# Attention and mixture of experts of a first layer, from two programs one after the other to one program of interleaved steps

## The reference, cut to what matters

```python
h = _layernorm(x) * (1 + ca) + sa
x = x + ga * attention0(h)      # 16 heads of 8, rope, causal, softmax, output projection
h = _layernorm(x) * (1 + cb) + sb
x = x + gb * ffn0(h)

def ffn0(x):                    # 32 experts of 64, top 6, and a shared one of 128
    shared = (silu(x @ shared_gate_w.T) * (x @ shared_up_w.T)) @ shared_down_w.T
    rw = softmax(x @ router_weight.T)
    combine = the 6 largest of rw + e_score_bias, rw there over their sum, else 0
    gate, up = split(einsum('th,eih->tei', x, gate_up_proj))
    y = einsum('tei,ehi->teh', silu(gate) * up, down_proj)
    return einsum('teh,te->th', y, combine) + shared
```

## Time and profile before

| | us |
|---|---|
| median of 3 runs | 1315.09 (1312.11 to 1319.2) |
| the profiled execution's own time | 1318.88 |
| its span, first to last instruction | 1317.0 |
| TensorE busy | 1017.9 (77%) |
| VectorE busy | 827.5 (63%) |
| ScalarE busy | 481.6 (37%) |
| GpSimd busy | 386.9 (29%) |

### The profile page before, as it was taken

How to read it: one execution, slowest core, us unless ns; L and a number is a source line. 1 busy time by engine, 2 the same in 40 slices (tenths; PEclk the granted TensorE clock), 3 DMA queues, 4 the chain that set the end, 5 groups by cost and what they waited for, 6 DMA issues and landing times. The chain is left out here.

```text
span 1317.0 us, 25195 instructions
## 1 busy us (share of the span) xinstructions
PE 1017.9 (77%) x9122; PEld 615.3 (47%) x9153; DVE 827.5 (63%) x1910; ACT 481.6 (37%) x839; POOL 386.9 (29%) x475
## 2 busy tenths in 40 slices
PE   3667878787878699999999997588988898844230
PEld 2333434343434344444444443377777777734120
DVE  4556666766651566667666654498889898566222
ACT  0024444444444233323323321465665565311110
POOL 4336454645522100000000001443333331016436
PEclk9998888888886699999999999589999999855575
DMA  4884656565620722321422230333322322040232
GB/s 120 215 153 76 133 89 130 90 124 95 128 47 2 245 81 89 106 91 66 127 91 78 92 107 23 97 99 99 87 72 91 99 71 79 1 128 33 75 110 77
DMA packets 86037, 125.69 MB, mean 95 GB/s; under 512 B 10170, under 2 KB 54128, under 8 KB 82176
## 3 DMA queue, kind: packets, MB, share of 16 engines
q1 hardware_dynamic: 83888, 120.98, 35.6%
q0 software_dynamic: 2048, 3.37, 0.9%
HBM read 92.50 MB, written 32.65 MB: 95 GB/s over the span
## 5 line engine op out<-in xcount | busy, mean ns | idle before, releaser
L473 ACT ACTIVATE a_pr<-ps 128x512 f32<-128x512 f32 x192 | 113.2, 597 | 161.6 <-PE ps L541 160.8
L922 ACT ACTIVATE e_sg<-ps 128x512 f32<-128x512 f32 x136 | 81.2, 597 | 245.2 <-PE ps L947 235.3
L734 DVE TENSOR_REDUCE a_nmax<-ps 128x2 f32<-128x512 f32 (+1 forms) x192 | 128.7, 686 | 55.8 <-PE ps L552 54.7
L1111 DVE TENSOR_TENSOR e_up<-e_sg,ps 128x512 f32<-128x512 f32 x128 | 87.9, 687 | 107.2 <-PE ps L954 101.3
L947 PE MATMUL ps<-e_hT,e_wg 128*128 128x512 f32 x272 | 141.3, 601 | 0.8 <-DVE e_wT L1098 0.8
L963 PE MATMUL ps<-e_hm,e_wd 128*128 128x512 f32 x272 | 139.2, 593 | 1.5 <-DVE e_pause L1109 0.8
L954 PE MATMUL ps<-e_hT,e_wu 128*128 128x512 f32 x272 | 139.8, 596 | 0.0
L508 PE MATMUL ps<-a_mask,identb 128*128 128x256 bf16 (+1 forms) x161 | 57.6, 358 | 68.3 <-DMA a_qs<-a_nparts_d 37.1
L1114 DVE TENSOR_TENSOR e_hm<-e_up,e_wb 128x512 f32<-128x512 f32 x128 | 88.5, 692 | 5.6
L541 PE MATMUL ps<-a_qs,a_ks 51*128 51x256 bf16 (+1 forms) x512 | 85.1, 276 | 6.0 <-ACT a_pr L473 1.5
L552 PE MATMUL ps<-a_ks,a_qs 48*128 48x256 bf16 (+1 forms) x512 | 87.7, 280 | 1.2 <-DVE a_nmax L734 0.7
(11 more groups left out here) (264 smaller groups left out, 2085.4 us busy)
## 6 DMA issues: line engine op xcount, KB each, us to landing
e_wb<-e_wT_d SPq DMA_DIRECT2D x128, 256.0 KB, 3.3
a_gw<-a_gd_d SPq DMA_DIRECT2D x16, 1024.0 KB, 4.9
a_qs<-a_terms_d SPq DMA_DIRECT2D x32, 384.0 KB, 5.4
a_ks<-a_terms_d SPq DMA_DIRECT2D x32, 384.0 KB, 7.1
a_gd_d<-a_gc SPq DMA_DIRECT2D x64, 132.0 KB, 2.4
a_terms_d<-a_parts SPq DMA_DIRECT2D x32, 192.0 KB, 2.2
a_terms_d<-a_parts SPq DMA_DIRECT2D x32, 128.0 KB, 2.1
a_terms_d<-a_parts SPq DMA_DIRECT2D x32, 64.0 KB, 1.8
```

What stands on the lines that cost most here:

```text
L473: nc.scalar.activation(dst, src, ACT.Exp).then_inc(exp_done, 1)
L734: nc.vector.tensor_reduce(dst, src, AX_X, ALU.max, negate=True).then_inc(m_read, 1)
L922: nc.scalar.activation(sg[:, par], ps[:, 2 + par], ACT.Silu).then_inc(silu_done, 1)
L1111: nc.vector.tensor_tensor(up[:, par], sg[:, par], ps[:, 4 + par], ALU.mult).then_inc(up_done, 1)
```

## The change

`attention0` and `experts0` become one stage, `first_layer`, fully unrolled: bodies -5 to 20. Attention keeps its body per batch. An iteration c of the experts spans an even and an odd body (U at body // 2 - 2, so bodies 2c + 4 and 2c + 5); its router (R) runs in body 2c + 3, its end (V) in body 2c + 6. Each engine has one list for even bodies and one for odd ones, woven from twelve slots, one for each score step: the slot's score step, then `first`, then the attention's other steps, then `second`.

```diff
+    M_BANK, C_BANK, O_BANK, A_BANK, D_BANK, G_BANK, U_BANK, Y_BANK = range(8)
+    OWN = 3
+    LAST = 2 * NI + 5
...
+        def m_bank(g, n, body):
+            return (M_BANK, G_BANK)[(3 * g + n) % 2] if body < OWN else M_BANK
+
+        def c_bank(g, n, body):
+            return (C_BANK, U_BANK)[(3 * g + n) % 2] if body < OWN else C_BANK
...
+            ahead = {"D": -1, "B": 0, "C": 0, "M": 1, "N": 2, "S": 2, "A": 4, "L": 5}
+            for body in range(-5, LAST):
+                for stage, step in (even, odd)[body % 2]:
...
+                        c = {"U": body // 2 - 2, "V": body // 2 - 3, "R": body // 2 - 1}[stage]
...
+        def weave(slots, first, second):
+            out = []
+            for i, (scores, others) in enumerate(slots):
+                out += scores + first.get(i, []) + others + second.get(i, [])
+            return out
```

The row maxima go from SBUF to SBUF, and SP's order changes:

```diff
-                sp.dma_start(nparts_d, nparts[:]).then_inc(nstored, 16)
-                sp.wait_ge(nstored, b.x * 16 + 16)
-                sp.dma_start(qs[TOP:TOP + 3, b.k % 3], nparts_d.rearrange("(t h) n -> t h n", h=H)).then_inc(nspread, 16)
-
-            run(sp, [("S", spread_again), ("M", spread_max), ("A", spread_parts)])
+                for t in range(3):
+                    sp.dma_start(qs[TOP + t:TOP + t + 1, b.k % 3], nparts[H * t:H * t + H]).then_inc(nspread, 16)
+
+            order = [("M", spread_max), ("S", spread_again), ("A", spread_parts)]
+            run(order, order)
```

On ScalarE, Silu of a unit's gates g becomes a copy g / 2 and tanh(g / 2), and the router's weights are stored and spread from ScalarE's queue:

```diff
-                    nc.scalar.activation(sg[:, par], ps[:, 2 + par], ACT.Silu).then_inc(silu_done, 1)
+                    act.wait_ge(gates_full, c.x * UNITS + u + 1)
+                    hold(act, hidden_done, UNITS, c, u - 1)
+                    nc.scalar.activation(half[:, par], ps[:, G_BANK], ACT.Copy, scale=0.5).then_inc(halved, 1)
+                    hold(act, up_done, UNITS, c, u - 1)
+                    nc.scalar.activation(th[:, par], ps[:, G_BANK], ACT.Tanh, scale=0.5).then_inc(gate_read, 1)
...
+                    act.wait_ge(w_stored, c.x * 16 + 16)
+                    hold(act, hidden_done, UNITS, c, u - RING + (1 if u > RING else 0))
+                    act.dma_start(wb[:, (u - 1) % RING], wT_d[c.k % 2, 2 * u - 2:2 * u].unsqueeze(0).to_broadcast([I0, 2, MT])
+                                  ).then_inc(w_spread[(u - 1) % RING], 16)
```

VectorE makes three products of a unit in place of two, (tanh + 1) * up, that by g / 2, and that by the weight:

```diff
+                    v.wait_ge(gate_read, c.x * UNITS + u + 1)
+                    v.wait_ge(ups_full, c.x * UNITS + u + 1)
+                    nc.vector.scalar_tensor_tensor(up[:, par], th[:, par], 1.0, ps[:, U_BANK], ALU.add, ALU.mult
+                                                   ).then_inc(up_done, 1)
+                    v.wait_ge(up_done, c.x * UNITS + u + 1)
+                    hold(v, down_done, UNITS, c, u - 1)
+                    if u == 0:
+                        nc.vector.tensor_tensor(hm[:, par], up[:, par], half[:, par], ALU.mult).then_inc(hidden_done, 1)
                         return
-                    nc.vector.tensor_tensor(up[:, par], sg[:, par], ps[:, 4 + par], ALU.mult).then_inc(up_done, 1)
+                    nc.vector.tensor_tensor(gw[:, par], up[:, par], half[:, par], ALU.mult).then_inc(weighted, 1)
+                    v.wait_ge(w_spread[(u - 1) % RING], c.x * 32 + 16 * ((u - 1) // RING) + 16)
+                    v.wait_ge(weighted, c.x * PAIRS + u)
+                    nc.vector.tensor_tensor(hm[:, par], gw[:, par], wb[:, (u - 1) % RING], ALU.mult
```

TensorE's gates wait for `gate_read` of the unit before (one bank), its ups for `up_done` of the unit before (one bank). From body 3 on each score step waits for `exp_done` and `m_read` of the one before. The new lists of TensorE and VectorE (G gates, U ups, Y down; the attention's slots keep their steps):

```diff
+            run(weave(slots,
+                      {0: [G[0], down("V", 15), U[0]], 1: [G[1], down("V", 16), U[1]], 2: [G[2]], 3: [U[2]],
+                       4: [Y[1]], 5: [G[4]], 6: [U[4]], 7: [Y[3]], 8: [G[6], ("V", return_tokens)], 9: [U[6]],
+                       10: [Y[5]], 11: [G[8]]},
+                      {2: [Y[0]], 3: [G[3]], 4: [U[3]], 5: [Y[2]], 6: [G[5]], 7: [U[5]], 8: [Y[4]], 9: [G[7]],
+                       10: [U[7]], 11: [Y[6], U[8]]}),
+                weave(slots,
+                      {0: [G[9]], 1: [U[9]], 2: [("R", take_tokens), Y[8]], 3: [G[11], ("R", route)], 4: [U[11]],
+                       5: [Y[10]], 6: [G[13]], 7: [U[13]], 8: [Y[12]], 9: [G[15], ("R", turn_weights)], 10: [U[15]],
+                       11: [Y[14]]},
+                      {0: [Y[7]], 1: [G[10]], 2: [U[10]], 3: [Y[9]], 4: [G[12]], 5: [U[12]], 6: [Y[11]], 7: [G[14]],
+                       8: [U[14]], 9: [Y[13]], 10: [G[16]], 11: [U[16]]}))
...
+            run(weave(slots,
+                      {3: [hidden(2)], 6: [hidden(4)], 8: [("V", token_residual)], 9: [hidden(6)]},
+                      {0: [hidden(0)], 1: [hidden(1)], 4: [hidden(3)], 7: [hidden(5)], 10: [hidden(7)],
+                       11: [hidden(8)]}),
+                weave(slots,
+                      {1: [hidden(9)], 3: [("R", logits)], 4: [hidden(11)], 6: [("R", top_eight)], 7: [hidden(13)],
+                       8: [("R", weights)], 9: [("R", take_weights)], 10: [hidden(15)]},
+                      {0: [("R", token_statistics), ("R", moments)], 1: [("R", token_normalise)], 2: [hidden(10)],
+                       4: [("R", softmax)], 5: [hidden(12)], 6: [("R", replace_six)], 7: [("R", chosen)],
+                       8: [hidden(14)], 10: [("U", take_gate)], 11: [hidden(16)]}))
```

More of the change, by code:

```diff
@@ new lines, in gated @@
+            def gated(c):
+                act.wait_ge(down_done, c.x * UNITS + UNITS)
+                act.wait_ge(gate_done, c.x + 1)
+                hold(act, e_back, 1, c, 0)
+                for k in range(HALVES):
+                    a = nc.scalar.activation(e_yo[:, k * L:(k + 1) * L], ps[:, Y_BANK, k * L:(k + 1) * L], ACT.Copy,
+                                             scale=gb[:, k:k + 1])
+                a.then_inc(sum_read, 1)
+            slots = [([("C", exps(i // 3, i % 3))], []) for i in range(UN)]
@@ L523, in step @@
                         pe.wait_ge(m_spread, b.x * SPREAD + SPREAD)
[L524 to L525 removed]
+                    hold(pe, m_read, UN, b, 3 * g + n - (1 if body < OWN else 0))
+                    bank = ps[:, m_bank(g, n, body)]
                     if n < 2:
@@ new lines, in down, with step @@
+            def down(stage, u):
+                def step(c):
+                    pe.wait_ge(hidden_done, c.x * UNITS + u + 1)
+                    if u == 0:
+                        hold(pe, sum_read, 1, c, 0)
+                    nc.tensor.matmul(ps[:, Y_BANK, :], wd[:, u, :], hm[:, (c.k + u) % 2, :],
+                                     start=(u == 0), stop=(u == UNITS - 1), skip_group_check=True
+                                     ).then_inc(down_done, 1)
+                return (stage, step)
@@ new lines, in _ @@
+            ahead = (("M", 2), ("M", 3), ("N", 0), ("N", 1))
+            slots = [([("B", scores(i // 3, i % 3, *ahead[i // 3]))], []) for i in range(UN)]
+            slots[2][1].append(("D", outputs(3)))
+            slots[2][1].append(("S", project_values))
+            slots[3][1].append(("D", turn_outputs(0)))
+            slots[4][1].append(("A", turn_tokens))
+            slots[5][1].append(("C", outputs(0)))
+            slots[5][1].append(("D", turn_outputs(1)))
+            slots[6][1].append(("D", turn_normal))
@@ new lines, in top_eight, with replace_six @@
+            def top_eight(c):
+                at = Count(c.x * E_DVE + 9)
+                v.wait_ge(dve_e, at.now())
+                nc.vector.memset(e_pause[:], 0.0)
+                for k in range(K):
+                    nc.vector.max(top[:, k, :], cor[:, k, :]).then_inc(dve_e, at.up())
+            def replace_six(c):
+                at = Count(c.x * E_DVE + 13)
+                v.wait_ge(dve_e, at.now())
+                nc.vector.memset(top[:, :, TOP_K:8], NEG).then_inc(dve_e, at.up())
+                v.wait_ge(dve_e, at.now())
+                nc.vector.memset(e_pause[:], 0.0)
+                for k in range(K):
+                    nc.vector.match_replace(rep[:, k, :], top[:, k, :], cor[:, k, :], -NEG).then_inc(dve_e, at.up())
@@ L1122, in residual @@
-            def residual(b):
-                v.wait_ge(o_full, b.x + 1)
-                xs = x[:, bass.ds(b.x * K, K), :]
-                nc.vector.tensor_tensor(xs, xs, ps[:, 1, :].rearrange("p (k d) -> p k d", d=D), ALU.add
-                                        ).then_inc(o_read, 1)
-            run(v, between([hidden(u) for u in range(UNITS)],
-                           [(0, "A", statistics), (1, "A", moments), (2, "A", normalise), (3, "O", residual),
-                            (6, "A", logits), (7, "A", softmax), (8, "A", top_eight), (9, "A", replace_six),
-                            (10, "A", chosen), (11, "A", weights), (13, "A", take_weights),
-                            (16, "U", gate)]))
+                return ("U", step)
@@ new lines, in _ @@
+            slots = [([("M", maxima(2 + i // 3, i % 3))], []) for i in range(6)]
+            slots += [([("N", maxima(i // 3, i % 3))], []) for i in range(6)]
+            slots[2][1].append(("S", values))
```

(6 more changed lines are left out.)

628 lines of the change are left out of this document (282 added, 346 removed).

## The result

The changed kernel takes 1306.72 us in the median of 6 runs (1303.16 to 1310.94), the kernel before 1314.87 (1312.11 to 1319.2); the ratio is 0.9938, with an interval of 0.9911 to 0.9966. The gain of 8.2 us is real and is a fifth of the 37 us forecast (1315 to 1278); the time lies inside the range, near the case without a change. The experiments ran in three later groups; the kernel before, run beside each, had medians of 1315.52, 1314.42 and 1314.69, so medians of different groups are compared here to about 1 us.

What follows compares the result with a forecast made beforehand. It took TensorE to bound the experts and waits the attention. 81 + 3 x 18 + 26 + 356 + 156.5 + 98 + 4 gave 775.5 against 817.8; with 2 for loads, 1317.0 became 1276.7, around the span 1278 us (1243 to 1338).

Steps and rivals of the forecast that it cites:

- the case without a change: Rival between the others: mixed bodies of 47.5 to 48.5 us, about 1315 us in all, within 0.5%; chance 0.07.
- joined stretch: Bodies holding attention and experts: 44.5 us a full mixed body, eight make 356; VectorE and TensorE 83 to 90% busy.
- body 0's first exponential: Ramp of the first attention: direct transfer of the row maxima gains 5 us (0 to 9), so body 0 starts at 81.
- bodies 0 to 2: Attention alone: 22.2 less 3.4 of waiting and about 1 for slow clock, 18 us each (15.5 to 20).
- body 3: Attention plus the first router, 7.4 us of VectorE work in long chains, and single banks: 26 us.
- The 3.4 us taken off: TensorE's wait per attention body for row maxima coming back from DRAM, 37.1 us in 11 waits, taken as removed.
- The cost of VectorE: Mixed bodies: added products bring VectorE from 65% busy to equal with TensorE, 38.9 us against 38.6 a body.
- The new product: VectorE's scalar_tensor_tensor at 512 columns in the experts: taken as 0.76 us, between 0.69 and 0.97.
- GpSimd beside VectorE: Mixed bodies: VectorE products with two SBUF inputs wait for GpSimd instructions, 2.2 us a body, 1.5 on the path.
- The loads of the second experts' weights: Seven issues and some 1.6 MB moved into the second attention: 2 us, between 0 and 8.
- The end: Bodies 12 to 15 at 156.5 us, four bodies of experts alone at 24.5 each, 98 in all, then 4.
- The slow rival: VectorE and GpSimd in each other's way: 51 us a mixed body, 1346 us, deciding from 47.9 on; chance 0.22.

Runs made afterwards that it cites:

- direct transfer alone: Kernel before, stages still separate, with row maxima moved by three direct SBUF transfers ahead of `spread_again` instead of through DRAM: 1300.64 us, ratio 0.9879.
- the last joined kernel: Changed kernel with earlier statistics, `rstd` and `normalise`, later `take_tokens`, and `keep(3)` put ahead of `split_rest` on GpSimd: 1266.69 us, ratio 0.9646.

## Why the prediction was wrong

Its sign and its joined stretch were right, its gain was not. Step by step, us:

| step | forecast | measured |
|---|---|---|
| body 0's first exponential | 81 | 81.1 |
| bodies 0 to 2 | 54 | 69.4 |
| body 3 | 26 | 34.7 |
| bodies 4 to 11 | 356 | 358.4 |
| bodies 12 to the layer's end | 258.5 | 262.3 |
| end of the first layer | 775.5 | 805.9 |

(Bodies are measured from one first `keep` to the next, 83.83, 153.22, 187.94 and 546.34; the last row also holds the 2.7 us from 81.1 to 83.83. Such a `keep` comes behind three exponentials, and so behind the wait at the start of its body. From first exponential to first exponential, 81.09, 145.27 and 181.22, bodies 0 to 2 take 64.2 and body 3 36.0.)

- **The step that failed: "Bodies 0 to 2, attention alone: 22.2 - 3.4 - about 1 for the slow clock = 18."** It took the wait out and asked nothing about what came next. Half of the 30 us missing are here (15.4). The chain `rotate(1)`, `split_parts`, `rstd`, `normalise`, maxima was as long as the round trip and hidden by it; direct transfer alone left the body at 22.2. Behind that chain lay the one to `keep(3)`. With both removed the body is 18.8: the 18 was near the truth for a kernel that the change did not make. For the joined lists I walked VectorE and TensorE in their orders; for these bodies, and for GpSimd's order anywhere, I did not.
- **The 3.4 us taken off was too much as well.** It is the mean of the 11 waits of the earlier trace rows, and one of them is the 9.2 us of the ramp; the other ten are 27.9 us, 2.8 each, in 15 bodies. The same view shows TensorE waiting 26 times for the maxima of VectorE, and in one body, at 107.66, for the 3.84 us that the changed kernel has.
- **Body 3, 26 us, was mis-sized for a reason of its own.** With the three waits moved (the last joined kernel) bodies 0 to 2 take 58.7 us, 10.7 less, but body 3 still 33.2. So of its 8.7 us only 1.5 hang on the step above. The sum added 7.4 us of VectorE's router work to 18 and had no term for TensorE, which is busy 29.9 of the 34.7 us at clock 0.71, and 28.3 of 33.3 at 0.74 in that last kernel. Which part is the clock, the single banks or the router's chain these runs do not separate.
- **The joined stretch was right**, 44.8 us a body against 44.5, with both engines and the clock as said. The wait of `take_tokens` is up to 2.6 us there (2.7 forecast).
- **The cost of VectorE** was right in kind: equal with TensorE, and the third product worth 49.7 us. What I did not draw from it is that this gives back all that the overlap wins over the direct transfer alone. Four runs show it: direct transfer alone -14, Tanh with three products +18 with the programs apart, and the joined kernel at 1301 with Silu and at 1307 with Tanh, neither ahead of the 1301 of the direct transfer alone.
- **The new product** at 512 columns was forecast at 0.76; of 136, none took over 0.69. Of the bounds, 0.69 and 0.97, the lower one was true.

```profile
L1101 DVE SCALAR_TENSOR_TENSOR a_up<-a_th,ps x136: 655/687/690, 184.3 to 800.0; 128x512 f32<-128x512 f32 x136
```

- **GpSimd beside VectorE** was right: the two products with both inputs in SBUF take 692 ns in the median and up to 1398 and 1462; their means are 773 and 870 in bodies 4 to 11 and 692 from 700 to 800, where GpSimd is busy 1.2 of 100 us.

```profile
L1108 DVE TENSOR_TENSOR a_gw<-a_up,a_half x128: 691/692/1398, 187.6 to 800.7; 128x512 f32<-128x512 f32 x128
```

  The first, with one input in PSUM, never exceeds 690. By the Trainium skill ("SBUF — State Buffer", Who interferes with whom) just that one should be free of GpSimd; the trace agrees, in 136 against 256 products.
- **The loads of the second experts' weights**, 2 us forecast: hardly seen in the spread of the second layer (1 us in the mean). The unrolled program, at nothing: no run shows a cost.
- **The end**: bodies 12 to 15 took 151 us (156.5 forecast), the rest 109 (102). The last routers have no attention beside them, and TensorE waits for their tokens and others of their steps (697 to 806):

```profile
PE ps L840 <- DVE a_e_y L1013: 3.4, 1, 3.4
PE ps L860 <- DVE a_up L1101: 1.8, 1, 1.8
```

The slow rival named the right pair of engines and too high a price: 44.8 us a body is under its point of 47.9. That the result came near "no change" is not that rival's doing, since it wanted 47.5 to 48.5 in the mixed bodies.

## What to carry over

When a wait is removed, write down for every engine, GpSimd too, what it does during that wait and what stands behind it in its order; the chain that the wait covered may be as long, and a second behind it. A body in which the wait happens to be absent shows that chain before anything is changed. Here three such waits, taken out one after the other by one transfer and four moved steps, gave 54 us with the stages apart (1260.74), and the joined kernel with the same steps and `take_tokens` moved was no faster (1266.69). What an overlap costs on the engine that it fills is to be weighed against what it wins: the joined kernel was 43.6 us ahead without its third product, and with that product, or with ScalarE's loads in its place, it was not ahead at all. Compare with simply filling the gaps of the stage that waits.

## What the chip showed unexpectedly

A change of ScalarE's table costs ScalarE its load and little else: 142 loads of 1283 ns in 360 us, with 49 us in which ScalarE was idle, at most 0.35 for each load. The Trainium skill ("ScalarE: Activation LUTs", What ACT_TABLE_LOAD costs) states 2.66 us for a switch with its drain; 142 of those, by that figure, would be 378 us, more than the stretch, so here the measurement decides: 1.28.

TensorE's granted clock differs between bodies of the same work: 0.84 where 4.2 of 21.8 us are idle, in waits of up to 2.6 us, and 1.00 where 3.1 of 18.8 are, in waits of at most 1.3 us. That is part of the price of a wait: of the 3.0 us by which the second body is shorter, 1.1 are idle time and 1.9 TensorE's busy time for the same matmuls.
